# An attention and expert kernel on one core: the sign pass of batch 0 ahead of the next score copies, head 12 copied behind a clamp, and a 23rd place in the ring of expert weights

## The reference

```
x = x + _layernorm(_L0_attn_ref(_layernorm(x), key_param, Wq, bq, Wk, bk, Wv, bv, Wo, bo))
x = x + _layernorm(_L0_ffn_ref(_layernorm(x), slot_query, d_*, c_*, e_*))

# attention: 16 heads of 16, 32 keys made from key_param, for each of the 2 x 2048 rows
scores = einsum('blhe,bshe->bhls', queries, keys)
A = sparsemax(scores / 4)          # max(z - tau, 0), sum 1 over the 32 keys of a head
out = einsum('bhls,bshd->blhd', A, values) @ Wo + bo

# experts: 16 slots attend over the 2048 rows of x (d_*), one slot for each of 16 experts
o = q + _mha(q, x, x, d_*)
h = _layernorm(o) * g + b
u = silu(h @ e_W1[e] + e_b1[e]);  g = silu(h @ e_Wg[e] + e_bg[e])     # 256 x 1024 each
o = o + (u * g) @ e_W2[e] + e_b2[e]                                    # 1024 x 256
out = _mha(x, o, o, c_*)           # every row attends over the 16 slots of its batch
```

## Times and profile before

| | us |
|---|---|
| runs, median of 3 | 463.04 |
| lowest, highest | 462.29, 465.19 |
| the profiled execution | 461.39 |
| its span | 459.7 |
| TensorE matmul busy | 397.7 |
| VectorE busy | 310.2 |
| ScalarE busy | 225.3 |
| GpSimd busy | 147.3 |

### The profile page before, as it was taken

The page is one execution under the profiler, slowest core; times in us unless marked ns, Lnnn a source line. Parts: engine busy times, 40 slices in busy tenths (PEclk is TensorE's granted clock), DMA queues, the critical chain, the costliest instruction groups (busy, mean ns, idle before and its releaser), DMA issues. The chain is left out here.

```text
span 459.7 us, 6977 instructions
## 1 busy us (share of the span) xinstructions
PE 397.7 (87%) x2086; PEld 245.7 (53%) x2086; DVE 310.2 (67%) x1189; ACT 225.3 (49%) x413; POOL 147.3 (32%) x243
## 2 busy tenths in 40 slices
PE   7987757589799988999999898999998679999983
PEld 4543223235455454665867666634443237888872
DVE  4899899989999986675425324333334125979996
ACT  2445746748778787878575633100000010355761
POOL 4134465482957522333212100010000000345353
PEclk9997787979989998999999899999999899999999
DMA  7931011011010228448539936979999999701215
GB/s 246 289 124 46 1 46 46 1 46 48 1 46 3 75 97 280 147 151 285 185 135 324 364 139 218 365 249 400 385 404 377 397 378 344 282 0 47 85 54 183
DMA packets 45055, 83.78 MB, mean 182 GB/s; under 512 B 2007, under 2 KB 36445, under 8 KB 40797
## 3 DMA queue, kind: packets, MB, share of 16 engines
q1 hardware_dynamic: 44722, 83.16, 51.7%
q10 hardware_dynamic: 298, 0.21, 0.2%
HBM read 70.78 MB, written 12.58 MB: 181 GB/s over the span
## 5 line engine op out<-in xcount | busy, mean ns | idle before, releaser
L1135 PE MATMUL bank<-Wz,yT 128*128 128x512 f32 x128 | 70.3, 701 | 19.1 <-DVE top L1739 18.9
L1135 PEld LDWEIGHTS bank<-Wz,yT 128*128 128x128 f32 x128 | 27.9, 226 | 54.7 <-issue 44.9
L1739 DVE MAX8 top<-bank 128x8 f32<-128x32 f32 x512 | 51.6, 178 | 1.3 <-ACT arena L798 1.1
L1071 ACT ACTIVATE d<-d 128x32 f32<-128x32 f32 x16 | 3.7, 229 | 84.7 <-DVE d L2127 84.7
L1168 PE MATMUL bank<-aWo,hoT 128*128 128x256 f32 x128 | 37.0, 412 | 0.2 <-DVE arena L1885 0.2
L738 POOL TENSOR_TENSOR work<-work 128x512 f32<-128x512 f32 x16 | 16.6, 1059 | 63.1 <-DVE work L2202 63.1
L1231 PE MATMUL bank<-d,work 128*128 128x256 f32 x128 | 31.9, 397 | 1.6 <-ACT d L897 1.6
L629 POOL TENSOR_SCALAR veps<-mv 128x4 f32<-128x4 f32 x24 | 5.9, 244 | 78.6 <-DVE mv L1659 53.7
L1591 PE MATMUL bank<-scr,work 128*128 128x256 f32 x128 | 29.1, 381 | 1.6 <-ACT work L1084 1.6
L1202 PE MATMUL bank<-arena,Wd 128*128 128x512 f32 x64 | 29.2, 599 | 1.5 <-ACT arena L869 1.5
L1567 PE MATMUL bank<-scr,arena 128*128 128x256 f32 x128 | 28.9, 380 | 0.0
(11 more groups left out here) (295 smaller groups left out, 880.6 us busy)
## 6 DMA issues: line engine op xcount, KB each, us to landing
arena<-in_L_ffn_e_W_dram SPq DMA_DIRECT2D x10, 1024.0 KB, 8.4
x<-in_L_ffn_e_W_dram SPq DMA_DIRECT2D x7, 1024.0 KB, 6.3
scr<-in_L_ffn_e_W_dram SPq DMA_DIRECT2D x7, 1024.0 KB, 13.7
arena<-in_L_ffn_e_Wg_dram SPq DMA_DIRECT2D x6, 1024.0 KB, 9.7
work<-in_L_ffn_e_W_dram SPq DMA_DIRECT2D x5, 1024.0 KB, 12.5
x<-in_L_attn_query_dram SPq DMA_DIRECT2D x1, 4096.0 KB, 16.5
out_dram<-x SPq DMA_DIRECT2D x8, 512.0 KB, 4.4
away_dram<-arena SPq DMA_DIRECT2D x8, 512.0 KB, 8.0
```

The costliest lines, as they stand in the source:

```text
L1135: mm = pe.matmul(bZ[t % 2][:, :], yT[:, c, t * P:(t + 1) * P], Wz[:, c, :], start=(c == 0), stop=(c == C - 1))
L1739: mx = v.max(top[:, h * TG + t, :], bZ[t % 2][:, h * NS:(h + 1) * NS])
```

## The change

Three things are changed, and the first of them moves some buffers and transfers.

- The ring gets a 23rd place, MIXERS, place 13: four quarters in `Wz[:, 1]`, `hoT`, `aWo` and `top`. The places behind it move up by one (PIECES is the former QUARTERED, now 18). Since Wk, Wv and Wo of the last attention used to lie in the first three of these, they are now loaded behind the last expert load, and `hcol` moves from `top` to `xin`, where the expert biases were; it is cleared when those have been transposed (`turned`).
- In batch 0, ScalarE's sign pass over group i stands ahead of the first two score copies of group i + 2.
- In the last group, ScalarE's copy of head 12 stands behind the clamp of the first half.

```diff
-        places_x = [0, 3, 8, 14]
-        places_y = [9, 5, 11, 16]
-        QUARTERED = 17
-        slots_of.insert(QUARTERED, None)
+        places_x = [0, 3, 8, 15]
+        places_y = [9, 5, 11, 17]
+        MIXERS, PIECES = 13, 18
+        slots_of.insert(MIXERS, None)
+        slots_of.insert(PIECES, None)
         R = len(slots_of) + 1
...
-        hcol = top[:, :, :].rearrange("p r k -> p (r k)")[:, 0:192].rearrange("p (q c x) -> p q c x", q=EB, c=C)
+        hcol = xin[:, 3, 0:192].rearrange("p (q c x) -> p q c x", q=EB, c=C)
...
-        quarters = (extra[:, :], past[:, 0:512], Wd[:, :, :].rearrange("p c n -> p (c n)"), spare[:, 512:1024])
+        quarters = {PIECES: (extra[:, :], past[:, 0:512], Wd[:, :, :].rearrange("p c n -> p (c n)"), spare[:, 512:1024]),
+                    MIXERS: (Wz[:, 1, :], hoT[:, :, :, :].rearrange("p q m n -> p (q m n)"),
+                             aWo[:, :, :].rearrange("p c d -> p (c d)"), top[:, :, :].rearrange("p r k -> p (r k)"))}
...
             sp.dma_start(abo, A['L0_attn_bo'].rearrange("(o d) -> o d", o=1).broadcast_to([P, D])).then_inc(abo_in, 16)
-            mixer(cWk, 'L0_ffn_c_Wk', "(p c) n -> p c n")
             spill(1)
...
             sp.wait_ge(o_ps, 2 * KT)
             fetch(12)
-            mixer(cWv, 'L0_ffn_c_Wv', "(p c) n -> p c n")
-            mixer(cWo[:, :, :], 'L0_ffn_c_Wo', "(c p) n -> p c n")
+            fetch(13)
             sp.wait_ge(x_new, NG)
-            fetch(13)
+            fetch(14)
...
+            emptied(MIXERS)
+            mixer(cWk, 'L0_ffn_c_Wk', "(p c) n -> p c n")
+            mixer(cWv, 'L0_ffn_c_Wv', "(p c) n -> p c n")
+            mixer(cWo[:, :, :], 'L0_ffn_c_Wo', "(c p) n -> p c n")
             fetch_back(0)
...
             roots(2, 7)
+            pool.wait_ge(turned, 1)
             pool.memset(hcol, 0.0).then_inc(consts, 1)
...
                 put_yT(i + 2)
+                signs(i, 0)
                 put_scores(i + 2, 0, range(2))
-                signs(i, 0)
...
             second_norm(1)
+            clamp(7, range(1))
             take_h(12)
-            clamp(7, range(1))
             take_o(11)
```

More of the change, by code:

```diff
@@ L211, in place_quarter @@
         def place_quarter(n, c, k):
-            if n % R == QUARTERED:
-                return quarters[2 * c + k]
+            if n % R in quarters:
+                return quarters[n % R][2 * c + k]
             return place_half(n, c)[:, 512 * k:512 * k + 512]
@@ L527, in _ @@
             unused(3)
-            fetch(14)
+            fetch(15)
             sp.wait_ge(g_ps, KT // 2 + KT // 4)
-            fetch(15)
+            fetch(16)
             send_away(7)
             left(3)
-            fetch(16)
+            fetch(17)
             sp.wait_ge(turned, 1)
             sp.wait_ge(h_ps, 2 * KT)
-            fetch(17)
+            fetch(18)
             sp.wait_ge(pT_ps, KT)
-            fetch(18)
             fetch(19)
+            fetch(20)
             sp.wait_ge(g_ps, KT)
-            fetch(20)
+            fetch(21)
             sp.wait_ge(dve_part, PREP + 2 * MS)
-            fetch(21)
+            fetch(22)
             for n in range(R, 3 * NE):
@@ L921, in _ @@
             put_yT(4)
+            signs(2, 0)
             put_scores(4, 1, range(2))
-            signs(2, 0)
             clamp(3)
@@ L1464, in weights @@
                 n = turn_of[e, k]
-                pe.wait_ge(e_in[n % R], {QUARTERED: 64, R - 1: 32}.get(n % R, 16) * (n // R + 1))
+                pe.wait_ge(e_in[n % R], {MIXERS: 64, PIECES: 64, R - 1: 32}.get(n % R, 16) * (n // R + 1))
                 return [[place_quarter(n, c, h) for h in range(2)] for c in range(2)]
```

## The result

The changed kernel takes **455.75 us** (median of 4 runs, 454.92 to 457.09) where the kernel before, measured beside it, takes 463.0 (462.29 to 465.19). The ratio is 0.9863 [0.9839, 0.9887] (95% interval), 1.4% or 6.3 us less; the two medians alone differ by 7.25 us.

A forecast was written before the change was run, and what follows sets the result against it. Bound by VectorE before 100 us and by full DMA engines in the experts; 461.39 - 2.7 (ring) - 1.1 (signs) = 457.6 us for the profiled execution, 463.04 - 3.8 = 459.2 for the median, range 457.0 to 462.3.

The forecast's parts named there:

- VectorE's new waits: Batch 0: VectorE's three waits for ScalarE before its sum would be 0.25, 0.25 and 0.5 us.
- the two sums of the last batch: Last batch: VectorE's waits before its two sums would be 0.7 and 0.75 us.
- the cover of 0.7 us for the mixers: At the fold: the mixer's weights, loaded last, would land about 378.2 us, 0.7 us before TensorE needs them at 378.9.
- Mixers late: Rival, chance 0.15: the mixer's three transfers need 1 to 3 us more than their bytes, giving 460.2 to 461.9 us.
- The clock falls in the fold: Rival, chance 0.08: TensorE drops to half clock in the fold through a wait for the mixers, costing 1.35 us: 460.6.
- The signs pay nothing: Rival, chance 0.12: VectorE's waits shrink but another engine takes them over before 180 us, giving 460.3 us.
- Part 4: Batch 0: ScalarE's sign pass ahead of the score copies shortens VectorE's three waits, -1.1 us, bounds 0 and 2.1.
- 463.04 - 3.8: Median forecast: median of before, 1.65 us above the profiled execution, less the summed gain of 3.8 us, giving 459.2.
- the second keeps its time: Batch 0, first turn: the first score copy ends by 47.7 us, the second score copy stays at its old time.
- Part 1: Experts' load ring: a 23rd place leaves 26 loads instead of 27 behind 302 us, -2.7 us at the mean rate.
- Part 5: Last group: head 12's copy behind the first clamp brings VectorE's first sum 0.27 us earlier; gain 0, at best -0.27.
- more than I count: Rival, chance 0.07: all of VectorE's waits go (2.1 us) and the load spacing is 2.9 us, giving 458.0 us.

The follow-up runs named there:

- e11: The changed kernel with the first return of ynT ahead of the mixer's three weights instead of behind them: 457.95 us, ratio 0.9925.
- e9: The kernel before with the new sign order in batch 0 and ten dummy products in TensorE's waits ahead of experts 13, 14 and 15: 457.9 us.
- e1: The kernel before with only ScalarE's sign pass moved ahead of the score copies in batch 0: 459.39 us, ratio 0.9932.
- e3: The kernel before with only the copy of head 12 moved behind the clamp: 461.95 us, ratio 0.9985.
- e2: The changed kernel with ScalarE's old order in both places, so ring, mixers and hcol alone: 459.23 us, ratio 0.9917.

## Why the prediction was wrong

**Right, by their rows.** VectorE's new waits, the two sums of the last batch, a gap ahead of the experts (somewhat shorter), 26 loads, 5.5 us of waiting in the experts for 5.8, nothing waiting at the fold, and the cover of 0.7 us for the mixers, which e11 measured. The sum made from the profile of before also fits the profile after in these places: -1.15 for -1.1 and -3.0 for -2.7. *Mixers late* didn't come; with the transfers moved, what it said would happen did, in place and size. *The clock falls in the fold* happened in e11 and e9, at 1.5 us for 1.35, in e9 without a wait for the mixers. *The signs pay nothing* is out by e1.

**Wrong: the step from the profiled execution to the median, and Part 4.** I took three waits from one execution and called their whole sum, 2.1 us, the upper bound, although these waits end a chain that hangs on TensorE's clock, which differs between executions. The profiled execution lay 1.65 us below the median, and I carried it over as a constant ("463.04 - 3.8"). But what that execution lacked was in part what the change takes away: waits of up to 3.4 us in batch 0, and 1.0 to 1.1 us in batch 1. By the profiles the order of the signs is worth 1.6 us in batch 0 and 1.0 in batch 1, 2.6 in sum; by e1's time 3.15, with 2.6 inside its interval. I had named this chain ("the second keeps its time") and not asked what happens when the product is later.

**Wrong in size: Part 1.** "By the mean rate that is 2.73 us", and I took -2.7. The mean is over loads of all kinds, nearly all in the full stream. The loads that matter are those behind the gap: 3.4 us on average by the last landing against the first expert product, 3.0 in the pair of before and after, and 3.2 by the bytes at the restart. My argument that all later landings come one load earlier was right; the price should have come from the landings behind 302 us, which the trace of before has.

**Part 5** was called nothing. e3 has it at -0.7 [-1.7, +0.3] us, so it can't be told from nothing.

**In sum:** 3.4 (ring) + 1.6 + 1.0 (signs) = 6.0 us, where 6.3 and 5.6 were measured by the ratios. The rival *more than I count* had the direction, but it too stopped at the waits of one execution.

## What to carry to other kernels

When a wait ends a chain that begins behind an idle TensorE, its length in one profile is a draw and no bound: look at a second execution, or ask how much later the first link can be, before a bound is put on what cutting the chain brings. A profile that is faster than the median is one in which something didn't happen, and the change may be aimed at just that. Price a transfer by the place where it leaves the stream, by its kind, and not by the mean rate of the stage; and look at the bytes moved beside the landings, since a late landing can be a matter of order.

## What the runs showed of the hardware that I had not expected

In a queue that stays full, loads of 1,048,576 bytes land 2.5 to 2.6 us apart where they move in packets of 8 KB (W1, Wg) and 2.9 us apart in packets of 1 KB (W2). The first load behind a gap takes 4.8 to 5.3 us whichever of Wg and W2 it is. A load's landing can lie behind 0.6 to 0.9 MB of later loads already moved (22 places, loads 24 and 25 at the landing of load 23).

TensorE's granted clock falls to 0.50 (1.2 GHz) behind the same idle gap in one execution and not in the next: at 126 us in six of the 17 profiles, and in the experts' waits between 354 and 380 us in all that have no dummies there, where it costs little if another wait follows (before and the changed kernel), and 1 to 2.4 us behind the last one (e1, e2, e3). The Trainium skill, "TensorE: Matmul & The Clock Gate" (Part 1: The HAM clock gate), has the point of the change vary between runs of one kernel; the traces agree, and show one such place moving this kernel of 460 us by about 1 to 2.4 us, above all where another engine's chain hangs on it.
